# Second attention layer: its heads in pairs on the two 64-row halves of the array, two products that add up in place of one of 97 or 99 rows

## The chip, the cores and the metric

The kernel runs on one core of a Trainium2 chip. The time is that of the whole program on the device, in microseconds, as the median of several runs. The profile is of one execution; its times are microseconds from the first instruction of the span.

## The reference, cut to what matters

Four layers follow each other, each added to the residual: two attention layers, a recurrent layer (GRU over 256 steps) and a last block. The input is 8 examples of 256 channels by 512 tokens for the attention layers. The changed code is in the second attention layer (8 heads of 32 channels, queries equal to keys):

```
q = xt @ Wq.T
qh = q.reshape(B, T, NH, dk).transpose(0, 2, 1, 3)
scores = scale * jnp.einsum('bhqd,bhkd->bhqk', qh, qh)
logits = (scores * cmask + (1.0 - cmask) * NEG) * rmask
attn = jax.nn.softmax(logits, axis=-1)
ctx = jnp.einsum('bhqk,bhkd->bhqd', attn, qh)
```

The first attention layer has 16 heads of 16 channels and is built in the same way.

## The kernel before

**Numbers in two parts.** Projections (q, k) are split into a high and a low part, so that a score is the sum of three products: high by high, high by low, low by high. These stand above each other as rows of one operand: 3 x 16 = 48 rows for a head of the first layer, 3 x 32 = 96 rows for one of the second. Mask rows follow (3 in the first layer, 1 in the second), and two rows that hold the negated row maximum in two parts. So the matrix product that finds the maxima has 51 or 97 rows, and that of the scores 53 or 99.

**Heads.** In the first layer two heads share an operand: one lies in rows 0 to 63 of the array, one in rows 64 to 127 (`head`, L522). In the second each head takes the whole height, one operand per head (`K1`, `Q1`, L54).

**Units.** Four heads are a unit: units 0 to 3 are the first layer, 4 and 5 the second. A unit has four steps for the maxima (each: 128 queries against 512 keys, four heads, function `max_`, banks `MX`) and four for the scores (`score`, banks `ST`). VectorE reduces each `MX` bank to its row maximum (L416), ScalarE takes exp of each `ST` bank into `pr` (L472), and then TensorE multiplies `pr` by the values (`av`, bank `AV`; in the second layer the denominators `DN` too). The maxima of a unit are turned to a row and sent by DMA into `Q0` or `Q1` before its scores begin.

**The order.** `at_slot` (L113) writes the order out by hand. One turn of the loop has 24 slots. Slot s does scores of unit s // 4 (units 4 and 5 of the example before), and maxima of the unit that is 7 slots ahead. So slots 1 to 8 have first-layer work alone, slots 9 to 15 first-layer scores with second-layer maxima, slot 16 second-layer work alone, slots 17 to 23 second-layer scores with first-layer maxima. A slot is: two scores, two maxima, the AV products of the slot before, then two scores, two maxima, and in some slots transposes (L590, L629), projections (L603), values (L615, L620) or the last product (L637).

**Banks.** Three `MX` banks go round among maxima, transposes and projections: TensorE waits until the user three places before is read (`walk.clear`). Three `ST` banks go round among scores: a score waits for the exp of three scores before (L553).

**Operands.** SP writes the parts to DRAM (`pieces`) and reads them back stacked (`stack`, L276): 12 loads for a first-layer unit, 6 for a second-layer one. The waits for them count in `STACK`.

Of the kernel before, what the change touches and what calls it, by code (L numbers as in the profile page):

```python
# [5 lines left out]
def attention_layers(nc, xT, K0, ident, to_clear, cleared, preload, preload_late, xt_in, x, mask, wq0, wk0, wv0, b0, wq1, wo1, ident_in):  # L6

    fp32 = mybir.dt.float32
    f32r = mybir.dt.float32r
# [3 lines left out]
    P = 128  # L13
# [4 lines left out]
    DH = (16, 32)  # L18
# [10 lines left out]

    PROD = (3 * DH[0], 3 * DH[1])  # L30
    MAXROWS = (PROD[0] + 3, PROD[1] + 1)
    ROWS = (MAXROWS[0] + 2, MAXROWS[1] + 2)
    with ExitStack() as ctx:  # L33
# [19 lines left out]
        Q0 = sb("Q0", [P, HEADS[0] // 2, T], f32r)  # L53
        K1 = sb("K1", [P, HEADS[1], T], f32r)  # L54
        Q1 = sb("Q1", [P, HEADS[1], T], f32r)
        SIDES = ("q0", "k0", "k1", "q1")
# [18 lines left out]
        any8, b8 = sb("any8", [B, 1]), sb("b8", [B, 1])  # L75
        rows8 = Q1[0:B]
        d_any = dram("d_any", [B, 1], fp32)
# [17 lines left out]
        stacked = [sem(f"stacked{w}") for w in range(NU)]  # L95
        STACK = [16 * (12 if L == 0 else 6) for L, g in UNITS]

# [132 lines left out]
        def _(sp):  # L230
# [26 lines left out]
            for h in range(2):  # L257
                ones_rows(K0[64 * h + MAXROWS[0]:64 * h + ROWS[0], :, :], HEADS[0] // 2)
            ones_rows(K1[MAXROWS[1]:ROWS[1], :, :], HEADS[1])
            sp.wait_ge(const, 48 + CONST)  # L260

# [14 lines left out]
            def stack(b, w):  # L276
# [11 lines left out]
                if L == 0:  # L288
                    for h in range(2):
                        of = slice(4 * g + h, 4 * g + h + 3, 2)  # L290
                        at, pair = 64 * h, slice(2 * g, 2 * g + 2)
                        put(K0[at:at + 2 * n, pair, :], kd[:, of, :])
                        put(K0[at + 2 * n:at + 3 * n, pair, :], kd[0:n, of, :])
                        put(Q0[at:at + n, pair, :], qd[0:n, of, :])
                        put(Q0[at + n:at + 3 * n, pair, :], qd[:, of, :])
                        put(K0[at + 3 * n:at + 3 * n + 3, pair, :], d_rows[b, 0:3, :].rearrange("r (a t) -> r a t", a=1).to_broadcast([3, 2, T]))
                        put(Q0[at + 3 * n:at + 3 * n + 3, pair, :], d_rows[b:b + 1, 3:4, :].to_broadcast([3, 2, T]))
                else:
                    of = slice(4 * g, 4 * g + 4)
                    put(K1[0:2 * n, of, :], kd[:, of, :])  # L300
                    put(K1[2 * n:3 * n, of, :], kd[0:n, of, :])
                    put(Q1[0:n, of, :], qd[0:n, of, :])
                    put(Q1[n:3 * n, of, :], qd[:, of, :])
                    put(K1[3 * n:3 * n + 1, of, :], d_rows[b:b + 1, 0:1, :].to_broadcast([1, 4, T]))
                    put(Q1[3 * n:3 * n + 1, of, :], d_rows[b:b + 1, 4:5, :].to_broadcast([1, 4, T]))

# [37 lines left out]
        def _(pool):  # L344
# [9 lines left out]
            def split_row(b, bank, u):  # L354
# [9 lines left out]
                for j in range(2):  # L364
                    pool.wait_ge(nm_split, 2 * n - 1 + j)
                    if L == 0:
                        r = MAXROWS[0] + j
                        to = Q0[r:r + 65:64, 2 * g:2 * g + 2, :]
                    else:
                        r = MAXROWS[1] + j  # L370
                        to = Q1[r:r + 1, 4 * g:4 * g + 4, :]
                    pool.dma_start(to.rearrange("r h t -> r (h t)").bitcast(fp32), nmp[:, q, j].bitcast(fp32)).then_inc(nm_dma[u], 16)
# [9 lines left out]
            def back(b, bank, L, m):  # L382
                if L == 0 and m == 0:
# [4 lines left out]
                    pool.tensor_tensor(o, o, yT[0][:], ALU.add).then_inc(y0_added, 1)  # L388
            pool.wait_ge(const, 48 + CONST)
            Walk(pool).run(dict(maxT=split_row, proj=proj, back=back))  # L390

        @block.vector
        def _(dve):
# [18 lines left out]
            def max_(b, bank, u, qb, i):  # L412
                wait(dve, mx_mm, "max", (u, qb, i), b)

                col = 8 * (i % 2) + 4 * (i // 2) + qb if UNITS[u][0] == 0 else 4 * i + qb
                dve.reduce_max(mx[:, u, col:col + 1], bank[:, :], AX.X).then_inc(mx_red, 1)  # L416
# [49 lines left out]
        def _(act):  # L466
# [35 lines left out]
            def values(b, bank, L, m):  # L502
                if b == 0 and L == 0:
                    act.wait_ge(const, 48 + CONST)
                wait(act, v_mm, "values", (L, m), b)
# [12 lines left out]
        def _(pe):  # L518
# [3 lines left out]
            def head(L, g, i, n):  # L522

                if L == 0:
                    return slice(64 * (i % 2), 64 * (i % 2) + n), 2 * g + i // 2
                return slice(0, n), 4 * g + i

            def max_(b, bank, u, qb, i):
# [4 lines left out]
                walk.clear()  # L533
                K, Q = ((K0, Q0), (K1, Q1))[L]
                r, h = head(L, g, i, MAXROWS[L])
                pe.matmul(bank[:, :], Q[r, h, tok(qb)], K[r, h, :], start=True, stop=True).then_inc(mx_mm, 1)  # L536

# [7 lines left out]
            def score(b, bank, w, kc, i):  # L545
# [3 lines left out]
                if kc == 0 and i == 0:  # L549
                    if b == 0:  # L550
                        pe.wait_ge(const, 48 + CONST)
                    pe.wait_ge(nm_dma[w], 32 * (b + 1))
                wait_count(pe, exped, n - 3)  # L553
                K, Q = ((K0, Q0), (K1, Q1))[L]
                r, h = head(L, g, i, ROWS[L])
                pe.matmul(ST[n % 3][:, :], K[r, h, tok(kc)], Q[r, h, :], start=True, stop=True).then_inc(st_mm, 1)  # L556

# [815 lines left out]
```

## Time and profile before

| what | value |
|---|---|
| median of 3 runs | 2021.22 us (2017.73 to 2022.86) |
| span of the profiled execution | 2018.8 us |
| TensorE busy in it | 1851.9 us (92%) |
| VectorE, ScalarE busy | 1146.6 us (57%), 797.0 us (39%) |
| last score product begins | 939.8 us |

### The profile page before, as it was taken

Reading aid. Unit: us, or ns where it says so; the run is one execution under the profiler, and the core shown is the slowest. Engines: PE = TensorE matmul, PEld = TensorE weight load, DVE = VectorE, ACT = ScalarE, POOL = GpSimd, SP = SyncE. Lnnn points to the kernel's source line nnn. Section 1 sums busy time; section 2 is a strip of 40 time slices with the busy share of each in tenths; the row PEclk is TensorE's granted clock in tenths of the full one; section 3 lists DMA queues with packets and bytes.
Section 4 is the critical chain, followed back from the end, with each engine's and each line's share of the span. In section 5 each row is a group of like instructions: output and inputs, shape, how many; then the busy total and the mean of one; then the engine's idle time right before and its main releaser. Section 6 shows DMA issues by size and latency. Waiting matters only on the chain. (4 is left out here: it accounts for less than half of the span.)

```text
span 2018.8 us, 85472 instructions
## 1 busy us (share of the span) xinstructions
PE 1851.9 (92%) x37678; PEld 1265.0 (63%) x37678; DVE 1146.6 (57%) x3363; ACT 797.0 (39%) x2195; POOL 391.1 (19%) x862
## 2 busy tenths in 40 slices
PE   5989999999999999988899999999999999999974
PEld 2334444444444444444898888888888888888761
DVE  4767575666666676632355555555555555555567
ACT  0556565656555555624222222222222222222224
POOL 0121212021211212110131122221222211222113
PEclk7899999999999999988999999999999999999995
DMA  5644433515161524040200000000000000000002
GB/s 143 225 136 140 121 110 96 140 54 172 56 172 49 170 72 122 2 147 14 101 13 12 12 12 12 10 8 12 13 12 13 6 11 12 13 12 12 5 3 84
DMA packets 65521, 127.65 MB, mean 63 GB/s; under 512 B 15545, under 2 KB 22201, under 8 KB 61556
## 3 DMA queue, kind: packets, MB, share of 16 engines
q1 hardware_dynamic: 62076, 121.35, 20.5%
q8 instruction: 296, 4.85, 1.0%
q0 software_dynamic: 3072, 0.82, 0.2%
q14 instruction: 77, 0.63, 0.1%
HBM read 77.56 MB, written 37.85 MB: 57 GB/s over the span
## 5 line engine op out<-in xcount | busy, mean ns | idle before, releaser
L416 DVE TENSOR_REDUCE mx<-MX 128x1 f32<-128x512 f32 x768 | 486.6, 684 | 200.1 <-PE MX L536 199.7
L962 PE MATMUL gate<-whh,state 128*8 128x128 f32 x16384 | 499.1, 273 | 65.4 <-DVE state L878 64.2
L962 PEld LDWEIGHTS gate<-whh,state 128*8 128x8 f32 x16384 | 424.2, 91 | 133.8 <-DVE state L878 130.2
L472 ACT ACTIVATE pr<-ST 128x512 f32<-128x512 f32 x768 | 411.8, 600 | 172.9 <-PE ST L556 172.5
L962 PE MATMUL pg<-whh,state 128*8 128x128 f32 x8192 | 273.6, 273 | 0.7 <-issue 0.7
L910 ACT ACTIVATE rg<-pre 128x32 f32<-128x32 f32 x256 | 58.8, 230 | 535.3 <-DVE pre L858 535.3
L856 DVE STREAM_TRANSPOSE trn<-gate 128x128 f32<-128x128 f32 x256 | 81.2, 317 | 330.5 <-PE gate L962 330.5
L536 PE MATMUL MX<-K,Q 51*128 51x512 f32 (+1 forms) x768 | 243.8, 463 | 15.3 <-DMA Q<-d_rows 9.9
L556 PE MATMUL ST<-Q,K 53*128 53x512 f32 (+1 forms) x768 | 243.0, 485 | 12.2 <-ACT pr L472 12.1
L556 PEld LDWEIGHTS ST<-Q,K 53*128 53x128 f32 (+1 forms) x768 | 99.5, 187 | 211.2 <-ACT pr L472 120.8
L962 PEld LDWEIGHTS pg<-whh,state 128*8 128x8 f32 x8192 | 226.0, 90 | 1.5 <-issue 1.4
L815 POOL TENSOR_TENSOR xT<-xT,state 128x32 f32<-128x32 f32 x256 | 67.0, 262 | 757.0 <-DVE state L878 757.0
L536 PEld LDWEIGHTS MX<-K,Q 51*128 51x128 f32 (+1 forms) x768 | 108.1, 192 | 104.2 <-DVE mx L416 44.4
L936 PE MATMUL pg<-xT,wih 128*32 128x128 f32 x4096 | 164.4, 272 | 5.5 <-issue 5.3
L878 DVE TENSOR_TENSOR_SCAN state<-by,state 128x48 f32<-128x48 f32 x512 | 104.7, 246 | 67.5 <-ACT by L915 67.1
L361 POOL TENSOR_TENSOR nmp<-nm,zero 16x128 fp32r<-16x128 f32 x48 | 21.5, 448 | 624.8 <-ACT nm L488 624.8
L572 PE MATMUL AV<-pr,va 128*17 128x512 f32 x1024 | 135.6, 601 | 1.0 <-ACT pr L472 1.0
L912 ACT ACTIVATE state<-pre 128x64 f32<-128x64 f32 x256 | 66.7, 261 | 163.9 <-DVE pre L867 163.9
L936 PEld LDWEIGHTS pg<-xT,wih 128*32 128x32 f32 x4096 | 108.6, 109 | 9.1 <-issue 8.6
L946 PE MATMUL gate<-wihZ,xT 128*32 128x128 f32 x2048 | 104.0, 273 | 1.8 <-PEq L33 1.4
L915 ACT ACTIVATE by<-trn 128x16 f32<-128x16 f32 x512 | 90.7, 224 | 23.1 <-DVE trn L870 1.5
L861 DVE STREAM_TRANSPOSE trn<-gate 128x128 f32<-128x128 f32 x256 | 81.0, 316 | 23.8 <-PE gate L962 0.2
(185 smaller groups left out, 1879.3 us busy)
## 6 DMA issues: line engine op xcount, KB each, us to landing
d_q<-hi_q SPq DMA_DIRECT2D x32, 256.0 KB, 3.4
d_q<-lo_q SPq DMA_DIRECT2D x32, 256.0 KB, 4.7
d_k<-hi_k SPq DMA_DIRECT2D x32, 256.0 KB, 3.7
d_k<-lo_k SPq DMA_DIRECT2D x32, 256.0 KB, 4.5
K<-d_k SPq DMA_DIRECT2D x64, 128.0 KB
Q<-d_q SPq DMA_DIRECT2D x64, 128.0 KB
K<-d_k SPq DMA_DIRECT2D x16, 512.0 KB
Q<-d_q SPq DMA_DIRECT2D x16, 512.0 KB
```

What stands on the lines that cost most here:

```text
L416: dve.reduce_max(mx[:, u, col:col + 1], bank[:, :], AX.X).then_inc(mx_red, 1)
L472: act.activation(pr[:, kc % 2, i], ST[n % 3][:, :], ACT.Exp, scale=SCALE[UNITS[w][0]]).then_inc(exped, 1)
L536: pe.matmul(bank[:, :], Q[r, h, tok(qb)], K[r, h, :], start=True, stop=True).then_inc(mx_mm, 1)
L556: pe.matmul(ST[n % 3][:, :], K[r, h, tok(kc)], Q[r, h, :], start=True, stop=True).then_inc(st_mm, 1)
L572: last = pe.matmul(AV[r, :], v, pr[:, kc % 2, i, :], start=kc == 0, stop=kc == KC - 1)
L856: dve.transpose(trn[:, R, :], psR[:, 0:P]).then_inc(s_tr, 1)
L861: dve.transpose(trn[:, N, :], psN[:, 0:P]).then_inc(s_tr, 1)
L878: dve.tensor_tensor_scan(state[:, 1 - q, W3 * a:W3 * a + W3], by[:, half(a)].rearrange("p c b v -> p (c b v)"), threes(q, a), 0.0, ALU.mul ...
L915: a.activation(by[:, half(z), :, 2], tr[Z][:, half(z)], ACT.Sigmoid).then_inc(s_z[z], 1)
L936: last = pe.matmul(gb[i % 2][32 * j:32 * j + 32, 0:TG * B], wih[:, n, i * P + 32 * j:i * P + 32 * j + 32], xT[:, n, TG * blk:TG * (blk + 1 ...
L946: last = pe.matmul(zb[32 * j:32 * j + 32, P * w:P * (w + 1)], xT[:, k, t0:t0 + 4, :].rearrange("p t b -> p (t b)"), wihZ[:, k, P * w:P * ( ...
L962: last = pe.matmul(bank[32 * j:32 * j + B, lo:hi], held[q][:, c, :], whh[:, c, o + lo:o + hi], start=first, stop=done)
```

## The change

The three products of a second-layer head no longer stand in one operand of 96 rows. `K1` and `Q1` have a new axis of two parts: part 0 holds 64 rows (two of the three products), part 1 holds 32 rows (the third), the mask row and the two rows of the maximum. Both parts of an even head lie in rows 0 to 63, those of an odd head in rows 64 to 127. A head's product is then two products that add up in the same bank: part 0 starts it, part 1 ends it. For a pair, the order is: part 0 of the even head, part 0 of the odd head, part 1 of the even, part 1 of the odd. When the even head's turn comes only its part 0 is issued; its part 1 follows behind the odd head's part 0, which waits for its own bank.

```
-    PROD = (3 * DH[0], 3 * DH[1])
+    PROD = (3 * DH[0], DH[1])
...
-        K1 = sb("K1", [P, HEADS[1], T], f32r)
-        Q1 = sb("Q1", [P, HEADS[1], T], f32r)
+        K1 = sb("K1", [P, 2, HEADS[1] // 2, T], f32r)
+        Q1 = sb("Q1", [P, 2, HEADS[1] // 2, T], f32r)
...
-        STACK = [16 * (12 if L == 0 else 6) for L, g in UNITS]
+        STACK = [16 * (12 if L == 0 else 14) for L, g in UNITS]
...
-            ones_rows(K1[MAXROWS[1]:ROWS[1], :, :], HEADS[1])
-            sp.wait_ge(const, 48 + CONST)
+                ones_rows(K1[64 * h + MAXROWS[1]:64 * h + ROWS[1], 1, :, :], HEADS[1] // 2)
+            sp.wait_ge(const, 64 + CONST)
...
-                    of = slice(4 * g, 4 * g + 4)
-                    put(K1[0:2 * n, of, :], kd[:, of, :])
-                    put(K1[2 * n:3 * n, of, :], kd[0:n, of, :])
-                    put(Q1[0:n, of, :], qd[0:n, of, :])
-                    put(Q1[n:3 * n, of, :], qd[:, of, :])
-                    put(K1[3 * n:3 * n + 1, of, :], d_rows[b:b + 1, 0:1, :].to_broadcast([1, 4, T]))
-                    put(Q1[3 * n:3 * n + 1, of, :], d_rows[b:b + 1, 4:5, :].to_broadcast([1, 4, T]))
+                    for h in range(2):
+                        of = slice(4 * g + h, 4 * g + h + 3, 2)
+                        at, pair = 64 * h, slice(2 * g, 2 * g + 2)
+                        put(K1[at:at + 2 * n, 0, pair, :], kd[:, of, :])
+                        put(K1[at:at + n, 1, pair, :], kd[0:n, of, :])
+                        for k in range(2):
+                            put(Q1[at + n * k:at + n * k + n, 0, pair, :], qd[0:n, of, :])
+                        put(Q1[at:at + n, 1, pair, :], qd[n:2 * n, of, :])
+                        put(K1[at + n:at + n + 1, 1, pair, :], d_rows[b:b + 1, 0:1, :].to_broadcast([1, 2, T]))
+                        put(Q1[at + n:at + n + 1, 1, pair, :], d_rows[b:b + 1, 4:5, :].to_broadcast([1, 2, T]))
...
-                K, Q = ((K0, Q0), (K1, Q1))[L]
                 r, h = head(L, g, i, MAXROWS[L])
-                pe.matmul(bank[:, :], Q[r, h, tok(qb)], K[r, h, :], start=True, stop=True).then_inc(mx_mm, 1)
+                if L == 0:
+                    pe.matmul(bank[:, :], Q0[r, h, tok(qb)], K0[r, h, :], start=True, stop=True).then_inc(mx_mm, 1)
+                    return
+
+                low = head(L, g, i, 64)[0]
+                pe.matmul(bank[:, :], Q1[low, 0, h, tok(qb)], K1[low, 0, h, :], start=True, stop=False)
+                if i % 2 == 0:
+                    held["max"] = bank
+                    return
+                other = head(L, g, i - 1, MAXROWS[L])[0]
+                pe.matmul(held["max"][:, :], Q1[other, 1, h, tok(qb)], K1[other, 1, h, :], start=False, stop=True).then_inc(mx_mm, 1)
+                pe.matmul(bank[:, :], Q1[r, 1, h, tok(qb)], K1[r, 1, h, :], start=False, stop=True).then_inc(mx_mm, 1)
```

`score` is changed in the same way, with `ST` in place of the held bank. The maxima's columns and the row DMA of POOL are now placed alike in both layers.

On TensorE, slots 14 and 15 (first-layer scores, second-layer maxima; the half B of slot 14, then the first scores and maxima of slot 15) stand before as

```order
L556 MATMUL ST0<-Q0,K0 128x512
L556 MATMUL ST1<-Q0,K0 128x512
L536 MATMUL MX2<-K1,Q1 128x512
L536 MATMUL MX0<-K1,Q1 128x512
L556 MATMUL ST2<-Q0,K0 128x512
L556 MATMUL ST0<-Q0,K0 128x512
L536 MATMUL MX1<-K1,Q1 128x512
L536 MATMUL MX2<-K1,Q1 128x512
L572 MATMUL AV<-pr,va 17x512 x4
```

and now, from the same place on TensorE, as

```order
L568 MATMUL ST0<-Q0,K0 128x512
L568 MATMUL ST1<-Q0,K0 128x512
L542 MATMUL MX2<-K1,Q1 128x512
L542 MATMUL MX0<-K1,Q1 128x512
L547 MATMUL MX2<-K1,Q1 128x512
L548 MATMUL MX0<-K1,Q1 128x512
L568 MATMUL ST2<-Q0,K0 128x512
L568 MATMUL ST0<-Q0,K0 128x512
L542 MATMUL MX1<-K1,Q1 128x512
L542 MATMUL MX2<-K1,Q1 128x512
L547 MATMUL MX1<-K1,Q1 128x512
L548 MATMUL MX2<-K1,Q1 128x512
```

Each pair of maxima has become four products, and the one that completes the even head's bank (L547) stands behind the odd head's first (L542). In slot 16 TensorE has second-layer scores and maxima; its half B, then the scores of slot 17, was

```order
L556 MATMUL ST2<-Q1,K1 128x512
L556 MATMUL ST0<-Q1,K1 128x512
L536 MATMUL MX1<-K1,Q1 128x512
L536 MATMUL MX2<-K1,Q1 128x512
L556 MATMUL ST1<-Q1,K1 128x512
```

and is now, on TensorE,

```order
L572 MATMUL ST2<-Q1,K1 128x512
L572 MATMUL ST0<-Q1,K1 128x512
L576 MATMUL ST2<-Q1,K1 128x512
L577 MATMUL ST0<-Q1,K1 128x512
L542 MATMUL MX1<-K1,Q1 128x512
L542 MATMUL MX2<-K1,Q1 128x512
L547 MATMUL MX1<-K1,Q1 128x512
```

The scores are doubled in the same order. On SP, the loads of one second-layer unit from DRAM stood as

```order
L286 DMA K1<-d_k1 64x2048
L286 DMA K1<-d_k1 32x2048
L286 DMA Q1<-d_q1 32x2048
L286 DMA Q1<-d_q1 64x2048
L286 DMA K1<-d_rows 1x4x512
L286 DMA Q1<-d_rows 1x4x512
```

and each half of the pair now has its own set on SP, this one twice per unit:

```order
L286 DMA K1<-d_k1 64x2x512
L286 DMA K1<-d_k1 32x2x512
L286 DMA Q1<-d_q1 32x2x512 x3
L286 DMA K1<-d_rows 1x2x512
L286 DMA Q1<-d_rows 1x2x512
```

Six loads have become fourteen, with rows of 2 KB pieces in place of 8 KB.

## Rows read from the trace of the kernel before

**Rows 1.** Groups of instructions by shape: second-layer scores and maxima.
```profile
L556 PE MATMUL ST<-Q,K 99*128 99x512 f32 x256 | 100.4, 472 | 2.7 <-ACT pr L472 2.7
L536 PE MATMUL MX<-K,Q 97*128 97x512 f32 x256 | 98.3, 467 | 1.4 <-DVE xT L462 0.7
```

**Rows 2.** Busy time by stretch: length, PE, PEld, DVE, ACT, POOL, clock, DMA.
```profile
453.00:563.00 110.00, 107.33 (x591) 47.47 (x588) 72.02 (x118) 63.17 (x123) 19.68 (x29) 1.00 0.39 111
...
901.00:909.00 8.00, 8.00 (x15) 3.68 (x15) 7.64 (x13) 0.27 (x1) 1.86 (x4) 0.52 0.01 2
```

**Rows 3.** Timeline (start, length, engine, line), slot 5, half A.
```profile
478.19 0.51 PE L556 MATMUL ST<-Q,K 53*128 53x512 f32 x2
...
478.54 0.39 PE L536 MATMUL MX<-K,Q 51*128 51x512 f32 x2
...
478.86 0.62 PE L572 MATMUL AV<-pr,va 128*17 128x512 f32 x4
```

**Rows 4.** Timeline, slot 0 half B and the next score.
```profile
456.18 0.51 PE L556 MATMUL ST<-Q,K 53*128 53x512 f32 x2
...
456.52 0.39 PE L536 MATMUL MX<-K,Q 51*128 51x512 f32 x2
...
456.75 0.39 PE L556 MATMUL ST<-Q,K 53*128 53x512 f32 x1
```

**Rows 5.** Timeline, slot 11 half B, slot 12 half A.
```profile
505.65 0.49 PE L556 MATMUL ST<-Q,K 53*128 53x512 f32 x2
...
506.08 0.73 PE L536 MATMUL MX<-K,Q 97*128 97x512 f32 x2
506.24 2.18 ACT L472 ACTIVATE pr<-ST 128x512 f32<-128x512 f32 x4 [0.98 <-PE ST L556]
506.62 1.93 DVE L416 TENSOR_REDUCE mx<-MX 128x1 f32<-128x512 f32 x3 [0.78 <-PE MX L536]
...
506.74 0.64 PE L556 MATMUL ST<-Q,K 53*128 53x512 f32 x2
...
507.97 0.62 PE L572 MATMUL AV<-pr,va 128*17 128x512 f32 x4
```

**Rows 6.** Timeline, slot 13 half B to slot 14's AV.
```profile
512.55 0.49 PE L556 MATMUL ST<-Q,K 53*128 53x512 f32 x2
...
515.29 0.62 PE L572 MATMUL AV<-pr,va 128*17 128x512 f32 x4
```

**Rows 7.** Timeline, TensorE, half B of slots 15 and 16, each to the next AV.
```profile
519.58 0.49 PE L556 MATMUL ST<-Q,K 53*128 53x512 f32 x2
...
521.73 1.05 PE L572 MATMUL AV<-pr,va 128*17 128x512 f32 x8
522.71 0.73 PE L556 MATMUL ST<-Q,K 99*128 99x512 f32 x2
...
524.90 0.64 PE L572 MATMUL AV<-pr,vb 128*32 128x512 f32 x4
```

**Rows 8.** Timeline, slot 23 half B, slot 0 half A.
```profile
561.95 0.73 PE L556 MATMUL ST<-Q,K 99*128 99x512 f32 x2
...
562.61 0.51 PE L536 MATMUL MX<-K,Q 51*128 51x512 f32 x2
...
563.89 0.50 PE L536 MATMUL MX<-K,Q 51*128 51x512 f32 x1 [0.19 <-DVE mx L416]
564.33 0.64 PE L572 MATMUL AV<-pr,vb 128*32 128x512 f32 x4
```

**Rows 9.** Timeline, end of the stage, scores without maxima.
```profile
871.29 0.96 PE L556 MATMUL ST<-Q,K 99*128 99x512 f32 x3
...
872.54 0.49 PE L556 MATMUL ST<-Q,K 99*128 99x512 f32 x1 [0.28 <-ACT pr L472]
873.02 0.64 PE L572 MATMUL AV<-pr,vb 128*32 128x512 f32 x4
```

**Rows 10.** Timeline of SP's queue, loads of a second-layer unit.
```profile
870.11 1.14 SPq L286 DMA_DIRECT2D K<-d_k x2
```

More of the change, by code:

```diff
@@ L75, in attention_layers @@
         any8, b8 = sb("any8", [B, 1]), sb("b8", [B, 1])
-        rows8 = Q1[0:B]
+        rows8 = Q1[0:B].rearrange("p a s t -> p (a s) t")
         d_any = dram("d_any", [B, 1], fp32)
@@ L370, in split_row @@
                         r = MAXROWS[1] + j
-                        to = Q1[r:r + 1, 4 * g:4 * g + 4, :]
+                        to = Q1[r:r + 65:64, 1, 2 * g:2 * g + 2, :]
                     pool.dma_start(to.rearrange("r h t -> r (h t)").bitcast(fp32), nmp[:, q, j].bitcast(fp32)).then_inc(nm_dma[u], 16)
@@ L388, in back @@
                     pool.tensor_tensor(o, o, yT[0][:], ALU.add).then_inc(y0_added, 1)
-            pool.wait_ge(const, 48 + CONST)
+            pool.wait_ge(const, 64 + CONST)
             Walk(pool).run(dict(maxT=split_row, proj=proj, back=back))
@@ L413, in max_ @@
                 wait(dve, mx_mm, "max", (u, qb, i), b)
-                col = 8 * (i % 2) + 4 * (i // 2) + qb if UNITS[u][0] == 0 else 4 * i + qb
+                col = 8 * (i % 2) + 4 * (i // 2) + qb
                 dve.reduce_max(mx[:, u, col:col + 1], bank[:, :], AX.X).then_inc(mx_red, 1)
@@ L503, in values @@
                 if b == 0 and L == 0:
-                    act.wait_ge(const, 48 + CONST)
+                    act.wait_ge(const, 64 + CONST)
                 wait(act, v_mm, "values", (L, m), b)
@@ L522, in head @@
             def head(L, g, i, n):
-                if L == 0:
-                    return slice(64 * (i % 2), 64 * (i % 2) + n), 2 * g + i // 2
-                return slice(0, n), 4 * g + i
+                return slice(64 * (i % 2), 64 * (i % 2) + n), 2 * g + i // 2
+            held = {}
             def max_(b, bank, u, qb, i):
@@ L550, in score @@
                     if b == 0:
-                        pe.wait_ge(const, 48 + CONST)
+                        pe.wait_ge(const, 64 + CONST)
                     pe.wait_ge(nm_dma[w], 32 * (b + 1))
                 wait_count(pe, exped, n - 3)
-                K, Q = ((K0, Q0), (K1, Q1))[L]
                 r, h = head(L, g, i, ROWS[L])
-                pe.matmul(ST[n % 3][:, :], K[r, h, tok(kc)], Q[r, h, :], start=True, stop=True).then_inc(st_mm, 1)
+                if L == 0:
+                    pe.matmul(ST[n % 3][:, :], K0[r, h, tok(kc)], Q0[r, h, :], start=True, stop=True).then_inc(st_mm, 1)
+                    return
+                low = head(L, g, i, 64)[0]
+                pe.matmul(ST[n % 3][:, :], K1[low, 0, h, tok(kc)], Q1[low, 0, h, :], start=True, stop=False)
+                if i % 2 == 0:
+                    return
+                other = head(L, g, i - 1, ROWS[L])[0]
+                pe.matmul(ST[(n - 1) % 3][:, :], K1[other, 1, h, tok(kc)], Q1[other, 1, h, :], start=False, stop=True).then_inc(st_mm, 1)
+                pe.matmul(ST[n % 3][:, :], K1[r, 1, h, tok(kc)], Q1[r, 1, h, :], start=False, stop=True).then_inc(st_mm, 1)
             def av(b, bank, w, kc):
```

## The prediction, made before the changed kernel was run

> **What bounds the kernel now.** I read the slices of the page, the groups of instructions by shape, the busy time by stretch, and then the timeline of single slots. The attention stage takes the first 940 us, the recurrent layer the rest, and only the first holds what is changed: 256 score products with 99 rows and 256 max products with 97 [rows 1]. In its steady part one turn of the loop takes 110.0 us, and TensorE is busy for 107.3 of them at the full clock, VectorE for 72.0 and ScalarE for 63.2 [rows 2]. So TensorE's own sequence ends nearly every wait; the question is what makes it up, and which wait stands close behind it.
>
> I call the two parts of a slot half A (two scores, two maxima, then the AV products) and half B (two scores, two maxima, then whatever else the slot has). Four facts come from the timeline.
>
> 1. Two products on the two 64-row halves start together and count as one group. In a row of groups of the same kind the first takes 0.34 us to the next start, and the last 0.32 before AV starts (478.19, 478.54, 478.86) [rows 3]. A third group in a row comes 0.23 after the second (456.52 to 456.75) [rows 4], which leaves no time for a load between the two: its weights were loaded meanwhile. So k groups take 0.20 + 0.23k.
> 2. A product with 97 or 99 rows costs the same 0.23 in a row of its kind, and again 0.20 where the kind changes. Two 53-row scores and two 97-row maxima take 0.43 + 0.66 = 1.09 (505.65, 506.08, 506.74) [rows 5]. The 0.20 is load and drain at the change from halves to full height.
> 3. A score's bank is free for TensorE 1.24 after its product starts: exp begins at 0.59 (505.65 to 506.24) and the second score of the next half, which wants that bank, starts late, its pair ending at 507.38, so at about 506.89 [rows 5].
> 4. A maximum's bank is free 1.29 after its product starts (the reduction begins 0.54 after, 506.08 to 506.62; the whole is 562.61 to 563.89, a wait for VectorE) [rows 5, 8]. Without a load in front, 0.43 stands for 0.54 and 0.48 for 0.59. Three reductions in a row take 1.93, so they follow each other at about 0.61 and the last frees its bank 0.74 after its start.
>
> The Trainium skill (TensorEngine Tiling, Key Properties) says that a change of tiling mode drains TensorE. The trace agrees: 0.43 against 0.23. By that rule alone this change is a clean gain, which is the first rival below.
>
> **What the change does on TensorE.** Both products of a second-layer head are now of the half-height kind, and four products make two groups, so 0.46 of array time stands where two full-height products had 0.46. Nothing is gained there. What goes is the changes of height next to first-layer products. Half A with scores and maxima of different layers: 0.34 + 0.23 + 0.32 = 0.90 in place of 1.09, **0.19 saved**. Where half B is followed by the next half A at once, two more changes go. Where it is followed by transposes or projections (128 rows), nothing goes on that side, since full height used to run into full height. Counted over the 24 slots of a turn, 22 changes go, 4.2 us.
>
> **What it delays.** The even head's second product is issued behind the odd head's first. So the even head's bank is complete one or two groups later, and the even head also waits for the odd head's bank. In the slots without other work between B and A this wait ends last. With S the start of B:
>
> - Slots 11, 12, 14 (first-layer scores, second-layer maxima). The first maximum is complete with its second product, which starts at S + 0.57; its reduction begins at 1.00, its bank is free at 1.75. The next half A needs that bank for its odd head, and then still 0.34 + 0.32, so AV starts at 2.42. Before: 507.97 - 505.65 = 2.32 [rows 5]. Loss 0.10, where the changes of height alone would give 0.6 (three of them); over the three slots 0.2, since one of them stands at 2.42 already.
> - Slot 13, with the finish transposes: the odd head wants the bank of B's second maximum, free at 1.00 + 0.61 + 0.74 = 2.35; with 0.66, 3.01 against 515.29 - 512.55 = 2.74 [rows 6]. Loss 0.27.
> - Slot 15: the odd second-layer score waits for exp until 1.24, its second product starts at 1.58, the two groups of maxima at 1.81 and 2.04, AV at 2.37; before 521.73 - 519.58 = 2.15 [rows 7]. Loss 0.22.
> - Slot 16: the first score of B is complete at 0.34, exp begins 0.82, bank free 1.47; second product 1.81, maxima 2.09, AV 2.41; before 524.90 - 522.71 = 2.19 [rows 7]. Loss 0.22.
>
> Sum: 0.91 lost. Gained: the halves A of slots 9, 10 and 11, 3 x 0.19, less 0.04 for a bank that comes later in slot 9: 0.53. In slots 17 to 23 the maxima are first-layer products, a pair complete at once, and now earlier (0.57 against 0.66). There the gain stands: slot 23 into 0 goes from 564.33 - 561.95 = 2.38 to 1.75 + 0.43 = 2.18 [rows 8], and slots 19 to 22 give one change of height each, 0.8 together. Slots 17 and 18 end on the chain of reductions, which starts earlier: about 0.2 and 0.3 by the same reading. Together 1.46. A turn gets 0.53 + 1.46 - 0.91 = **1.1 us shorter**. Slots 9 to 16 run like this in 7 turns (0.38 lost in each), 17 to 23 in 6: 2.7 - 8.8 = -6.1 us.
>
> **The end of attention.** Where no first-layer work is left, there are no changes of height to save, and the delays stay. Scores alone, half B into half A: 873.02 - 871.29 = 1.73 before, the last pair waiting for exp [rows 9]; after, bank free at 1.47, plus 0.34 and 0.32, 2.13. Seven such places, +2.9. Six other places with transposes or projections between scores, where full height ran into full height, get two changes, about 0.39 each with the later bank: +2.4. Slot 16 once more, +0.2. The last example's 28 maxima before its scores run alone, one per 0.61 of VectorE. A pair now takes 0.75 (reduction) + 0.54 (product) = 1.29 for two reductions of 1.22: +0.07 for each of 8 pairs. In 901 to 909 us the granted clock is 0.52 [rows 2], nearly the lower level of 1.2 GHz, where load and product take twice as long (an estimate: 0.86 for 0.54), so +0.39 for each of 6. With the rest of the slow stretch, +3.8. Sum +9.3 us.
>
> **DMAs and set-up.** A second-layer unit has 14 loads for 6, with the same bytes. Two such loads take 1.14 us of SP to issue [rows 10], so eight more are at most 4.6 us per unit. The data has 13 slots before it is read, and behind it on SP stand the next example's pieces, with as much. Only for the last example is it near: +0, up to +4 if it shows. One more load of constants at the start: 0 to +0.5.
>
> **Sum.** Span 2018.8 - 6.1 + 9.3 = 2022.0. The median of the runs is 2.4 above the span, so 2024.4. Bounds of the unknown: the array's overlap of four half-height products in a row is shown only with one product per bank, at 0.23 per group [rows 4]; if accumulating cost nothing more it is my number, if each added group cost 0.34, 256 x 0.11 = +28. The other end is the case in which no bank wait binds, the first rival.
>
> The second place where I weigh a rule: the Trainium skill (TensorE: Matmul & The Clock Gate, The mechanism) has weight loads overlap running products only where the row group differs. Even and odd halves alternate here, and each half's next load would wait for its own product: by that rule 0.34 per group, 2052 us. Rows 4 show 0.23 for just such a group, so I keep the rule as a small chance.
>
> **Rivals.**
> - *Only the changes of height count.* 22 x 0.19 = 4.2 us per turn in 6.5 turns, -27, and +2.4 at the end: 1997 us. For it: TensorE busy 107.3 of 110.0 [rows 2]. Against it: the waits for exp and for a reduction are there already [rows 5, 8], so there is little slack behind TensorE. Chance 0.20.
> - *Slower: the held head decides everywhere.* The even head is held until the odd head's bank is free, so any late bank costs 0.66 in place of 0.43 after it. If reductions or exps come some 0.3 us later than I reckon, it decides in all 15 slots of a turn in which a second-layer head stands. Each then loses what slots 11 to 16 lose in my sum, 0.91 / 6 = 0.15: 15 x 0.15 x 6.5 = +15, and +9 at the end, 2045 us. It decides from the point where the bank comes later than TensorE's own sequence (in slots 11 to 14 1.75 against 1.04; in slots 19 to 22 the bank is the earlier by some 0.3). For it speaks that 563.89 waits for a reduction even now [rows 8]; against it, that the maxima of slots 17 to 23 stay single products. Chance 0.20.
> - *Loads not pulled ahead:* 2052 us, 0.05.
>
> **How the numbers follow.** Forecast 0.55, its own range 2016 to 2034. The measurement tells a change from none at about 0.3%, 6 us. Faster: 0.20 from the first rival and 0.07 of the forecast. Slower: 0.25 from the last two and 0.08 of the forecast. Same: 0.40. The range reaches from the first rival's time to near the second's: 1999 to 2042.
>
> **What would show it.** Three groups in half A of slots 9 to 11 taking 0.90; odd-head products of slots 12 to 16 idle with VectorE as releaser, and a slot of 3.4 us where slot 11 to 12 had 3.3; slots 18 to 23 each 0.2 shorter; a turn of 108.9 us; the time from the last full turn to the end of attention 9 longer. A turn under 107 would say that the bank waits don't bind, one over 111 that the held head does; 0.34 between neighbouring groups would say that loads are not pulled ahead.

## The result, and the profile after

The changed kernel takes 2027.41 us (median of four runs, 2026.26 to 2027.44) against 2019.47 for the kernel before in four runs beside it (2013.76 to 2022.86): ratio 1.0045, interval 1.0026 to 1.0064. Twelve later runs on another chip gave 2021.02 against 2016.36 (ratio 1.0024, 1.0012 to 1.0036). It is slower, by 5 to 8 us. The forecast was 3 us slower, 2024.4. The profiled span grew from 2018.8 to 2025.6.

The time of an execution also goes with its mean granted clock, 0.966 to 0.972 here: over the 65 executions on the second chip, three kernels beside the kernel before, a straight line gives about 1.2 us less for each 0.001. At equal granted clock that line puts the changed kernel 3.5 us (give or take 1.2) above the kernel before. This is an estimate from the recorded clocks, and I use it again below.

I measure the loop by the start of each slot's AV products to the start of the next slot's, as medians of turns 2 to 6. (These are sums over some 120 starts in each trace, so they stand as a table and not as rows.) A cell is after minus before, in us; "n to n+1" is the stretch that holds half B of slot n and half A of slot n+1.

| stretch | 0 to 8, each | 8 to 9 | 9 to 10 | 10 to 11 | 11 to 12 | 12 to 13 | 13 to 14 | 14 to 15 | 15 to 16 | 16 to 17 | 17 to 0, each | turn |
|---|---|---|---|---|---|---|---|---|---|---|---|---|
| measured | 0.00 | -0.18 | -0.14 | -0.03 | +0.10 | -0.01 | +0.26 | +0.08 | +0.28 | +0.22 | -0.20 | -0.79 |
| forecast | 0 | -0.19 | -0.15 | -0.19 | +0.10 | 0 | +0.27 | +0.10 | +0.22 | +0.22 | -0.21 | -1.1 |

The turn went from 110.00 to 109.21. The profile of one turn, from the busy time by stretch (length, PE, PEld, DVE, ACT, POOL, clock, DMA), answers to [rows 2]; the second row lies in the maxima of the last example:

```profile
453.00:562.20 109.20, 106.13 (x657) 47.90 (x660) 72.18 (x120) 63.62 (x123) 19.81 (x29) 1.00 0.41 112
901.00:909.00 8.00, 7.26 (x22) 3.40 (x20) 5.93 (x10) 0.27 (x1) 2.00 (x4) 0.50 0.01 2
```

TensorE lost 1.2 us of busy time per turn, and the turn 0.8. In the second row TensorE is idle for 0.74 us of 8 where it was idle for none, and VectorE made 10 reductions where it made 13.

The groups of instructions by shape answer to [rows 1]: 256 starting products for maxima (L542) and for scores (L572), and half as many ending ones on each line, for the maxima of even (L547) and of odd heads (L548).

```profile
L542 PE MATMUL MX<-K,Q 64*128 64x512 f32 x256 | 82.0, 455 | 3.5 <-DVE mx L419 2.0 <-DVE xT L465 0.6
L572 PE MATMUL ST<-Q,K 64*128 64x512 f32 x256 | 73.8, 490 | 4.6 <-ACT pr L475 4.1
L547 PE MATMUL MX<-K,Q 33*128 33x512 f32 x128 | 57.7, 451 | 0.0
...
L548 PE MATMUL MX<-K,Q 33*128 33x512 f32 x128 | 52.8, 412 | 0.0
```

The waits before these products, 3.5 and 4.6 us in sum, are longer than the 1.4 and 2.7 of [rows 1].

The gain, in the timeline (start, length, engine, line) of the changed kernel, slot 9's half A: three groups of half-height products in 0.90 us (493.11 to 494.01), at 0.34, 0.23 and 0.33. The last two groups use the same two halves and add up in the same banks. The 0.23 between them leaves no time for a load after the first has run, and none for a price of accumulating.

```profile
493.11 0.50 PE L568 MATMUL ST<-Q,K 53*128 53x512 f32 x2
493.45 0.40 PE L542 MATMUL MX<-K,Q 64*128 64x512 f32 x2
493.68 0.40 PE L547 MATMUL MX<-K,Q 33*128 33x512 f32 x1
493.69 0.40 PE L548 MATMUL MX<-K,Q 33*128 33x512 f32 x1
494.01 0.62 PE L593 MATMUL AV<-pr,va 128*17 128x512 f32 x4
```

The loss, slot 11's half B and slot 12's half A, answers to [rows 5]:

```profile
503.94 0.50 PE L568 MATMUL ST<-Q,K 53*128 53x512 f32 x2
504.27 0.40 PE L542 MATMUL MX<-K,Q 64*128 64x512 f32 x2
504.50 0.39 PE L548 MATMUL MX<-K,Q 33*128 33x512 f32 x1
504.51 0.40 PE L547 MATMUL MX<-K,Q 33*128 33x512 f32 x1
504.75 0.92 PE L568 MATMUL ST<-Q,K 53*128 53x512 f32 x2
504.94 2.57 DVE L419 TENSOR_REDUCE mx<-MX 128x1 f32<-128x512 f32 x4 [0.76 <-PE MX L547]
505.18 1.01 PE L542 MATMUL MX<-K,Q 64*128 64x512 f32 x2
505.69 0.18 PEld L542 LDWEIGHTS MX<-K,Q 64*128 64x128 f32 x1 [0.33 <-DVE mx L419]
505.69 0.49 PE L547 MATMUL MX<-K,Q 33*128 33x512 f32 x1
506.02 0.40 PE L548 MATMUL MX<-K,Q 33*128 33x512 f32 x1
506.35 1.05 PE L593 MATMUL AV<-pr,va 128*17 128x512 f32 x8
```

The first reduction begins at 504.94, 1.00 after the half's start, since it wants the even head's second product, and the bank comes free at 505.69, 1.75 after. VectorE is the releaser there. From 503.94 to 506.35 it is 2.41, where [rows 5] have 2.32.

In the kernel before, the same place (507.31) looks as if it waited for a reduction too, but the times speak against it:

```profile
507.31 0.30 PEld L536 LDWEIGHTS MX<-K,Q 97*128 97x128 f32 x2 [0.24 <-DVE mx L416]
```

The idle 0.24 before this load is the 0.24 that stands before the first maxima of the half as well (506.08), where nothing is waited for, and the load comes 0.42 after the second score (506.89), as there. So before the change exp's bank ended the wait (1.24 after the half's start, then 1.08 to AV). Now a reduction does (1.75, then 0.66). The first reduction itself ends hardly later than before: 1.66 after the half's start then, 1.70 now. Without that wait the place would take 1.24 + 0.90 = 2.14, less than before; the kernel with short reductions, below, takes just that.

### The profile page after: what moved, and what is told of

Same layout as the page of the kernel before. It is cut to its first block and busy times, and to the rows that moved or that the text cites. A ratio compares the mean times of both kernels' runs of the same rounds, so it can differ in the third digit from the quotient of the medians.

```text
span 2025.6 us, 86625 instructions
## 1 busy us (share of the span) xinstructions
PE 1853.9 (92%) x38190; PEld 1271.9 (63%) x38190; DVE 1148.4 (57%) x3363; ACT 800.6 (40%) x2195; POOL 392.5 (19%) x862
## 5 line engine op out<-in xcount | busy, mean ns | idle before, releaser
L568 PE MATMUL ST<-Q,K 53*128 53x512 f32 x512 | 147.6, 488 | 13.2 <-ACT pr L475 11.5
L568 PEld LDWEIGHTS ST<-Q,K 53*128 53x128 f32 x512 | 56.8, 184 | 154.3 <-ACT pr L475 112.3
L538 PE MATMUL MX<-K,Q 51*128 51x512 f32 x512 | 138.1, 432 | 12.1 <-DMA Q<-d_rows 9.7
L538 PEld LDWEIGHTS MX<-K,Q 51*128 51x128 f32 x512 | 67.7, 192 | 42.1 <-DVE mx L419 21.7
```

Source lines behind the costliest of these rows:

```text
L538: pe.matmul(bank[:, :], Q0[r, h, tok(qb)], K0[r, h, :], start=True, stop=True).then_inc(mx_mm, 1)
L568: pe.matmul(ST[n % 3][:, :], K0[r, h, tok(kc)], Q0[r, h, :], start=True, stop=True).then_inc(st_mm, 1)
```

## The experiments

Kernels that share a chip share its runs of the kernel before: 2017.91 us for the first four, 2018.48 for the next four, 2016.36 for the last three. A kernel with one execution has a single time.

**Full height for the last two examples (late_full).** Six examples run as in the changed kernel, the last two as in the one before, in the same memory.

```
+                elif b >= LATE:
+                    for h in range(2):
+                        put(K1[0:2 * n, h, pair, :], kd[:, of, :]) ...
+                if b >= LATE:
+                    pe.matmul(bank[:, :], Q1[0:97, i % 2, h, tok(qb)], K1[0:97, i % 2, h, :], start=True, stop=True).then_inc(mx_mm, 1)
+                    return
```

> Halves for the first six examples, full height (97 and 99 rows) for the last two, whose scores run without first-layer maxima beside them. Theory (the end of attention loses because no change of height is left to save there, while the later banks stay): turns 2 to 6 stay at 109.2 us, slots 9 to 16 of turn 7 go back to before (0.4 off), and the 8.3 us that the end of the stage lost come back, so about 2018 to 2020, 3 to 5 us under the kernel before on the same chip. Rival (the end is longer for another reason, the loads or the set-up): it stays within 3 us of the changed kernel, 2024 to 2028.

2011.70 us in nine runs, ratio 0.9967 (0.9955 to 0.9979), 6.2 us under before: faster than both kernels. The turn is 109.16, and turn 7, in full height again from slot 8 on, is as before to 0.01 in each slot. Turn 1 to turn 7 takes 5.4 us less than before. So the two signs of the change are separate: the loop gains, the end loses, and the end can be given back. I had expected 3 to 5 us under the kernel before. The 0.8 beyond the loop's 5.4 seems to go with the clock: these nine runs had a mean granted clock of 0.9707, the kernel before beside them 0.9691, and at equal clock a straight line through this chip's runs leaves about 5.3.

**Without holding (unheld).** Each head issues its second product at once, behind its first; the queue reads even 0, even 1, odd 0, odd 1.

```
                 pe.matmul(bank[:, :], Q1[low, 0, h, tok(qb)], K1[low, 0, h, :], start=True, stop=False)
-                if i % 2 == 0:
-                    held["max"] = bank
-                    return
-                other = head(L, g, i - 1, MAXROWS[L])[0]
-                pe.matmul(held["max"][:, :], Q1[other, 1, h, tok(qb)], ..., start=False, stop=True)
                 pe.matmul(bank[:, :], Q1[r, 1, h, tok(qb)], K1[r, 1, h, :], start=False, stop=True)
```

> Each head issues its two products at its own turn, so the even head isn't held behind the odd one. Theory (an odd head needs two products one after the other behind its bank, whether the even one is held or not; the pairing saves a group): no slot of 11 to 16 gets shorter, and every half that TensorE bounds gets one group of 0.23 longer, 19 of them in a turn: a turn of about 113.6 us, 2050 us in all. Rival (the held head decides): slots 11 to 16 shorter by 0.1 to 0.3 each, a turn under 109, about 2018 us.

2016.50 us in one execution, and a turn of 109.26, each slot within 0.02 of the changed kernel: both expectations failed. The timeline of unheld shows why (L542 starts a head, L543 ends it):

```profile
515.48 0.19 PEld L542 LDWEIGHTS MX<-K,Q 64*128 64x128 f32 x2
515.71 0.40 PE L542 MATMUL MX<-K,Q 64*128 64x512 f32 x2
515.71 0.19 PEld L543 LDWEIGHTS MX<-K,Q 33*128 33x128 f32 x2
515.94 0.39 PE L543 MATMUL MX<-K,Q 33*128 33x512 f32 x2
```

Both starting products run at 515.71 and both ending ones at 515.94. The odd head's first product stands third in the queue and started before the second in it. The array fed its two halves each in its own order, so the order across heads that the change writes out by hand was made by the chip in any case. Where the odd head waits for a bank, unheld is even ahead: the even head's second product (L543, 516.97) runs before the odd head's first has loaded (L542, 517.12). The slot is no shorter for it.

```profile
516.97 0.40 PE L543 MATMUL MX<-K,Q 33*128 33x512 f32 x1
517.12 0.18 PEld L542 LDWEIGHTS MX<-K,Q 64*128 64x128 f32 x1 [0.20 <-DVE mx L419]
```

**The kernel without holding, timed (unheld_timed, unheld_again), and the changed kernel beside it (after_again).** The first timing was on the chip of the next four, the second beside the changed kernel.

> The kernel unheld again, timed: each head's two products at its own turn. Its one execution so far had the same turn (109.26 against 109.21 us) and 3.8 us less in the stretch of maxima alone, where a pair took 1.34 us at the half clock against 1.58 with the even head's second product behind the odd head's bank. Theory A (that wait is real and costs 3 to 4 us once per execution, and the rest of the 11 us between the two single executions is spread of the start and the recurrence): median 2019 to 2024, ratio 1.001 to 1.003, between before and the changed kernel. Rival (the order of the two products is worth nothing anywhere, and 2016.5 was one short execution): median 2025 or more, ratio 1.0035 or more. A second rival (all 11 us are the holding): 2016 to 2018, ratio under 1.0005.

2020.98 us in twelve runs, ratio 1.0011 (0.9999 to 1.0023): theory A's range, and neither rival's.

> The changed kernel itself, beside unheld on one chip, so that the two can be set against each other. Theory (holding the even head's second product costs 1.58 against 1.34 us per pair in the half-clock part of the maxima alone, 2 to 4 us per execution, and nothing elsewhere): ratio to before 1.002 to 1.005, and 2 to 4 us above unheld_again. Rival (the four runs at 2026 to 2027 us were by chance in the upper part of its spread, and the two kernels are the same): 1.000 to 1.002, within 1.5 us of unheld_again.

> Unheld beside the changed kernel on one chip: 2020 to 2022.5 us (1.0011 the last time), 2 to 4 us under after_again by the theory that holding has a price where maxima run alone; within 1.5 us of it by the rival.

After_again: 2021.02 in twelve runs, 1.0024 (1.0012 to 1.0036). Unheld_again: 2017.86 in twelve, 1.0004 (0.9994 to 1.0015). The absolute times are lower than I wrote for unheld_again, since the kernel before was 2.1 us quicker on this chip; the difference is 3.2 us, inside the expected 2 to 4. The intervals, 1.0012 to 1.0036 and 0.9994 to 1.0015, overlap a little. And the two sets of runs differ in the clock: its mean is 0.9684 for the changed kernel and 0.9703 for unheld. At equal granted clock the line of the first section leaves 0.8 us (give or take 1.4) of the 3.2. Level by level the sign is not even steady: at 0.968 the changed kernel took 2020.8 to 2021.1 and unheld 2021.8 and 2022.3, at 0.970 it was 2016.4 and 2017.4 against 2018.0 to 2018.4, at 0.972 it was 2017.3 and 2018.1 against 2013.8 to 2017.4. Whether unheld gets more clock because of its order or by chance no run tells. What the order does costs time in one place, the last example's maxima alone. First the changed kernel (VectorE and TensorE in the timeline):

```profile
902.22 0.79 PE L542 MATMUL MX<-K,Q 64*128 64x512 f32 x1 [0.20 <-DVE mx L419]
902.22 0.79 PE L547 MATMUL MX<-K,Q 33*128 33x512 f32 x1
902.81 0.62 PE L548 MATMUL MX<-K,Q 33*128 33x512 f32 x1
...
903.05 1.29 DVE L419 TENSOR_REDUCE mx<-MX 128x1 f32<-128x512 f32 x2 [0.29 <-PE MX L547]
...
904.64 1.29 DVE L419 TENSOR_REDUCE mx<-MX 128x1 f32<-128x512 f32 x2 [0.30 <-PE MX L547]
```

Then unheld_again, the same stretch:

```profile
898.67 6.70 DVE L419 TENSOR_REDUCE mx<-MX 128x1 f32<-128x512 f32 x10 [2.08 <-PE MX L543]
...
901.41 0.79 PE L542 MATMUL MX<-K,Q 64*128 64x512 f32 x1
902.01 0.62 PE L543 MATMUL MX<-K,Q 33*128 33x512 f32 x1
```

Held, the even head's second product sits in the queue behind the odd head's first, which waits for a bank; two reductions then run and VectorE idles 0.3, a pair in 1.58 to 1.59 us (903.05 to 904.64). Unheld, ten reductions run without a gap in 6.70, 1.34 a pair. The queue passes a product by for a busy half; it did not pass it by behind a product that waits for a semaphore. From the first to the last of the 32 reductions there it is 26.3 and 26.6 us in the two profiles of the changed kernel, 24.6, 25.0 and 24.9 in the three of unheld: 1.3 to 2.0 us for holding. The stretch around them, from AV to AV, does not show even that much cleanly. Against before it lasts 3.7 and 1.7 us longer in the two profiles of the changed kernel, 0.1 less, 2.8 and 3.1 longer in the three of unheld, and in the kernels whose maxima are at full height there it lies anywhere from 2.6 less to 1.2 more. The clock's falls to half come at other places in each (at 892.6 us in after_again, at 881.9 and 895.5 in unheld_again). So the price of a pair is shown, and 1.3 to 2.0 us for all of them; the 3.2 between the medians is not shown to be holding's.

**The two together, held off and full height at the end (late_full_unheld).** Edit: both of the above.

> The kernel that goes back to full height for the last two examples, and without holding: each head's two products at its own turn in the first six. Theory: holding costs only where maxima run alone, which is at full height here, so the time is within 1.5 us of late_full's 2011.7 (2010 to 2013.5; ratio 0.996 to 0.998) and the turn 109.2. Rival (holding costs in every turn, covered in the single profile by spread): 2009 or less.

2011.90 us in seven runs, ratio 0.9968 (0.9955 to 0.9980), against 0.9967 for late_full: holding costs nothing in the loop. It even gains a little: from turn 1 to turn 7 the three kernels that hold take 650.8 to 651.0 us, the four that don't 651.4 to 651.6.

**The scores alone in halves (scores_halves).** Maxima are one product over part 0, so their numbers aren't the reference's.

```
-                pe.matmul(bank[:, :], Q1[low, 0, h, tok(qb)], K1[low, 0, h, :], start=True, stop=False)
-                ... the second products
+                pe.matmul(bank[:, :], Q1[0:97, 0, h, tok(qb)], K1[0:97, 0, h, :], start=True, stop=True).then_inc(mx_mm, 1)
```

> Only the scores of the second layer run as two products on the two halves; its maxima are one product of 97 rows a head, whose operand stands in both halves' tiles but holds other numbers than the reference wants (same shape, same work), so the output is not the reference's. Theory (each edit pays for itself, and what the two edits share is the change of mode between scores and maxima of a half B): in slots 17 to 23 the change of mode between the layers' scores is gone with the scores alone, so -0.19 us a slot there, seven times; slots 9 to 15 as before, since there only maxima of the second layer run; slot 16 +0.4 to +0.6, a new change of mode between scores in halves and maxima at full height; turn -0.7 to -0.9 us. After the last turn's loop: seven slots of scores alone at +0.4 each, in the seventh turn's end and again in the eighth's, the maxima alone unchanged: the whole 1 us over before. Rival (the scores at halves give the gain and the maxima the loss, so scores alone win): 3 us or more under before.

**The maxima alone in halves (maxima_halves).** The same for the scores, `K1[0:99, 0, h, tok(kc)]` with `Q1[0:99, 0, h, :]`.

> Only the maxima of the second layer run as two products on the two halves; its scores are one product of 99 rows a head over other numbers than the reference wants (same shape, same work), so the output is not the reference's. Theory: slots 8 to 10 gain what they gained with both edits (-0.35 us together), slots 11 to 15 lose what they lost (+0.7), slots 17 to 23 are as before, slot 16 +0.2 or more; turn +0.4 to +0.8 us, the stretch of maxima alone at the end +3 to +4 us: the whole 6 to 10 us over before. Rival (the loss of slots 11 to 15 comes from scores and maxima together, not from the maxima): turn under 110.0 and slots 11 to 15 within 0.2 of before together.

| stretch | 8 to 11 | 11 to 15 | 15 to 16 | 16 to 17 | 17 to 0 | turn | runs |
|---|---|---|---|---|---|---|---|
| scores alone | 0.00 | +0.02 | +0.41 | +0.19 | -1.39 | -0.80 | 1.0011 (0.9999 to 1.0023) |
| maxima alone | -0.36 | +0.45 | +0.26 | +0.42 | 0.00 | +0.76 | 1.0053 (1.0033 to 1.0072) |
| both | -0.35 | +0.43 | +0.28 | +0.22 | -1.37 | -0.79 | 1.0024 (1.0012 to 1.0036) |

Medians 2019.82 (ten runs) and 2029.28 (four). The theory holds in each stretch of the loop, and both rivals fall. At the end it was less exact: the maxima alone grew by 5.8 in maxima_halves, above the expected 3 to 4, and by 1.2 in scores_halves, where they were expected unchanged. Both are single profiles of a stretch that varies by some 4 us among kernels with the same maxima. Scores pay in slots 17 to 23, maxima cost in 11 to 15. Only in slots 15 and 16 do the two interact: 0.60 and 0.68 alone, 0.50 together, so there a change of height that either edit alone puts in is taken out by the other. Scores_halves at slot 15's half B shows it: the maxima start 0.43 after the scores and the next scores 0.66 after those. In the changed kernel the same two steps take 0.33 and 0.48 (518.29, 518.62, 519.10).

```profile
517.93 0.50 PE L561 MATMUL ST<-Q,K 53*128 53x512 f32 x2
518.36 0.74 PE L541 MATMUL MX<-K,Q 97*128 97x512 f32 x2
519.02 0.64 PE L565 MATMUL ST<-Q,K 64*128 64x512 f32 x2
```

**Shorter reductions, before and after (short_before, short_after).** Each maximum is taken over 256 of 512 keys, so the maxima are those of half the keys. This frees each maximum's bank earlier and leaves TensorE's work as it is.

```
-                dve.reduce_max(mx[:, u, col:col + 1], bank[:, :], AX.X).then_inc(mx_red, 1)
+                dve.reduce_max(mx[:, u, col:col + 1], bank[:, 0:256], AX.X).then_inc(mx_red, 1)
```

> The kernel before with maxima over the first 256 of the 512 keys only (left out: the other half of the reduction). Theory: VectorE's reduction falls from 0.69 to about 0.4 us; a turn is bounded by TensorE and shrinks by 0.3 to 0.8 us (few waits for a reduction), the maxima that run alone at the end by some 5. About 2010 us. Rival (VectorE paces the turn): a turn shorter by 3 us or more.

> The changed kernel with the same short reduction (left out: the second half of the keys in the maxima). Theory (the maximum's bank ends slots 11 to 15): start of half B to the AV products falls from 2.42 to about 2.15 in slots 11, 12 and 14 and from 3.00 to about 2.6 in slot 13, slot 16 stays at 2.4 (it waits for exp), and a turn is 1.5 to 2.5 us shorter than that of the kernel before with the same short reduction, in place of 0.8. Rival (the four products themselves take the time): the start of B to AV stays over 2.35, the difference of the turns stays 0.8.

1979.03 and 1970.28 us in one execution each; turns of 105.77 and 103.82. With short reductions the change makes the turn 1.95 shorter where it made it 0.79 shorter. Against short_before, the stretches 11 to 12, 12 to 13 and 14 to 15 now gain 0.17, 0.20 and 0.18; with the full reduction they stood at +0.10, -0.01 and +0.08. Stretches 15 to 16 and 16 to 17 still lose 0.22 and 0.19, since there exp's bank decides. Short_after, slot 11's half B to the next AV, takes 2.14 for the 2.41 above:

```profile
473.13 0.50 PE L568 MATMUL ST<-Q,K 53*128 53x512 f32 x2
...
473.95 0.93 PE L568 MATMUL ST<-Q,K 53*128 53x512 f32 x2
474.38 0.73 PE L542 MATMUL MX<-K,Q 64*128 64x512 f32 x2
474.72 0.41 PE L547 MATMUL MX<-K,Q 33*128 33x512 f32 x1
474.96 0.39 PE L548 MATMUL MX<-K,Q 33*128 33x512 f32 x1
475.27 0.62 PE L593 MATMUL AV<-pr,va 128*17 128x512 f32 x4
```

My expectation for short_before, under 1 us a turn, was far off: 4.2. Most of it (2.4) lies in slots 1 to 7, where the change does nothing and which I had not read: VectorE decides there.

**The loads (before_loads14).** The kernel before, its second-layer units loaded by 14 DMAs of two heads for 6 of four heads.

```
-                    of = slice(4 * g, 4 * g + 4)
+                    for h in range(2):
+                        of = slice(4 * g + h, 4 * g + h + 3, 2)
+                        ... the same rows, two heads at a time
```

> The kernel before with nothing but its second layer's loads cut as the change cuts them: 14 loads a unit in pieces of two heads, for 6 in pieces of four, the same bytes to full-height tiles. Theory (the loads lie under 13 slots of other work and cost nothing): turn 110.0 us, no slot off by 0.03, median within 1.5 us of before, ratio 0.999 to 1.001. Rival (part of what the changed kernel loses at the start and at the end comes from eight more issues a unit on SP): ratio 1.001 to 1.002 and over, with the difference in the first turn or after the last one.

2014.98 us in twelve runs, ratio 0.9998 (0.9986 to 1.0010), turn 109.98. The loads cost nothing.

## Why the prediction was right in its sum and half wrong in a cause

**The changes of height saved: right.** Slots 17 to 23 gained 1.37 (forecast 1.46) and the halves A of slots 9 and 10 gained 0.18 and 0.14. Half A of slot 11 was priced at 0.19 and gave 0.03. That term I had summed by kind instead of reading its slot: the odd head's first product waits there for its bank, which a reduction frees at 502.24, so the second of the two loads ends only at 502.47. The even head's second product stands behind it. The half takes 1.07 (501.88 to 502.95), not 0.90. Rows of the changed kernel:

```profile
501.56 0.68 DVE L419 TENSOR_REDUCE mx<-MX 128x1 f32<-128x512 f32 x1
...
501.88 0.50 PE L568 MATMUL ST<-Q,K 53*128 53x512 f32 x2
501.99 0.48 PEld L542 LDWEIGHTS MX<-K,Q 64*128 64x128 f32 x2
...
502.23 0.56 PE L542 MATMUL MX<-K,Q 64*128 64x512 f32 x2
...
502.95 0.62 PE L593 MATMUL AV<-pr,va 128*17 128x512 f32 x4
```

**The later banks: right to 0.06 in each stretch.** Slots 11 to 16 lost 0.93 by the table, forecast 0.91. Slot 11 to 12 came out at 2.41 (forecast 2.42), slot 13's half B at 3.00 (3.01), slot 16's at 2.41 (2.41); slot 15's at 2.42 (2.37). The rows of 13, 15 and 16, which answer to [rows 6] and [rows 7], TensorE alone:

```profile
510.92 0.50 PE L568 MATMUL ST<-Q,K 53*128 53x512 f32 x2
...
513.92 0.62 PE L593 MATMUL AV<-pr,va 128*17 128x512 f32 x4
...
518.29 0.50 PE L568 MATMUL ST<-Q,K 53*128 53x512 f32 x2
...
520.71 1.05 PE L593 MATMUL AV<-pr,va 128*17 128x512 f32 x8
521.69 0.50 PE L572 MATMUL ST<-Q,K 64*128 64x512 f32 x2
...
524.10 1.06 PE L593 MATMUL AV<-pr,vb 128*32 128x512 f32 x8
```

Short_after shows the cause for the maxima's bank. For exp's bank in slots 15 and 16 there is only that the loss stays when reductions shrink, and that the second score's start stands where exp ends.

**But the cause that I named was half wrong.** I wrote that the even bank is late because its second product is issued behind the odd head's first. Unheld takes the issue order away and each slot stays as it was. What makes the bank late is that a head has two products in one half, one after the other, 0.23 apart. Late it is against a pair of single products at half height; against the full height of before it is only 0.04 later in slot 11, and the wait for it decides because the rest of the half has become shorter. The issue order adds to that only where the odd head waits for a bank and nothing else hides it, in the maxima alone.

**The end: right for the scores, in part by luck for the maxima.** Forecast +9.3, and +0.4 for turn 7's slots 8 to 16. From turn 7 to the last AV it is 161.3 us where it was 152.5: +8.8 (+7.4 in after_again). Scores alone lost 0.41 per place (forecast 0.40). The rows answer to [rows 9]: 2.13 from the half's start to AV (869.90 to 872.04), as forecast, for 1.73.

```profile
869.90 0.51 PE L572 MATMUL ST<-Q,K 64*128 64x512 f32 x2
...
871.38 0.49 PE L572 MATMUL ST<-Q,K 64*128 64x512 f32 x1 [0.52 <-ACT pr L475]
...
872.04 0.64 PE L593 MATMUL AV<-pr,vb 128*32 128x512 f32 x4
```

The maxima alone lost 3.7 (forecast 3.8) in the first profile and 1.7 in the second; a pair at the half clock takes 1.59 for 1.22, +0.37 where I had +0.39. So the pair's price was right. That the whole came to 3.7 is partly luck: 0.9 of the 3.8 was added for the rest of the slow stretch without a sum, and the same stretch varies by nearly 4 us among five kernels whose maxima are at full height.

**The loads: right**, at nothing.

**The total.** Turn 1 to turn 7 shrank by 5.2 (forecast 6 x 1.1 = 6.5), the end grew by 8.8, together +3.6. The span grew by 6.9. The other 3.3 are the start (turn 1 begins 1.4 later) and what follows attention (last AV to the end, 1.9 longer), which hold nearly nothing of the change. Before_loads14, unheld and late_full reach turn 1 at 131.1, 130.5 and 131.0 us, before at 132.5 and after at 133.8. That goes with the time that they run at the half clock until then: 37.5 us in those three, 41.0 before, 47.8 after. I had the change at +3.2. The twelve runs on one chip say +4.7 (1.0024 of 2016.36), and 3.5 at equal granted clock.

**The rivals.** *Only the changes of height count* (1997 us) fell: it wants every bank free in time, and even with short reductions the change gives 1.95 of the 4.2. *The held head decides everywhere* (2045 us) fell: slots 19 to 22 gained. *Loads not pulled ahead* (2052 us) fell at 0.23 between the groups at 493.45 and 493.68. The rule behind it, which the Trainium skill states (TensorE: Matmul & The Clock Gate, The mechanism), that a load overlaps only products of another row group, is not what this trace shows. The same section also lets a load into the background weight buffer run ahead, which I had passed over; that agrees with the loads of L543 at 515.71, while L542 runs on both halves.

## What to carry to other kernels

Splitting a product over rows into two that add up is free in array time when both find a partner on the other half, and buys the changes of height around it; but the result is complete one product later, so count for each such place who waits for the bank, and split only where TensorE itself is the last (here: in six of eight examples, 5 to 6 us under the kernel before in place of 5 over it). Sum such a gain place by place in the timeline, not by kind.

Don't put a second product of one head behind a first product of another that may wait for a bank: in the loop it bought under 0.1 us a turn, and where maxima ran alone it cost 1.3 to 2.0 us.

## What the runs showed of the hardware

Products of the two halves do not start in queue order: with the queue at even 0, even 1, odd 0, odd 1, the third started within 3 ns of the first and 0.23 us before the second (515.71 and 515.94 above). The Trainium skill (TensorE: Matmul & The Clock Gate, The mechanism) says that products start strictly in program order; this trace differs, and the turn of 109.26 us, where 113.6 was expected with a loss of 0.23 in each of 19 halves, agrees with the trace.

A product that waited for a semaphore did hold up those behind it, on the other half too (the 0.3 us of VectorE's idle time per pair at 903.05 and 904.64; at 505.69 the load of L542 waited for VectorE, and L547 on the other half started with it, while unheld ran that product ahead, 516.97 against 517.12).

With the maxima alone, a pair of full-height maxima at the half clock took 1.22 us before (eight reductions in 4.88 from 904.88 us), a pair of split ones 1.34 unheld and 1.59 held.
